# Attention loop of a macaron block on one core: the keys' correction, exponential, rounded half and remainder moved ahead of the queries' work on three engines

## The reference, cut to what matters

```python
x = x + 0.5 * ffn(layernorm(x))          # experts choose tokens: softmax over the tokens, top 8 per expert
x = x + attn(layernorm(x))
x = x + 0.5 * ffn(layernorm(x))

def attn(x):
    q, k, v = x @ Wq.T + bq, x @ Wk.T + bk, x @ Wv.T + bv      # split into 16 heads of 32
    q, k = exp(q), exp(k)
    kv = cumsum(k[:, :, :, None] * v[:, :, None, :], axis=1)
    k1 = cumsum(k, axis=1)
    num = einsum('zsD,zsDd->zsd', q, kv)
    den = sum(q * k1, axis=-1)
    return (num / den) @ Wo.T + bo
```

## Time and profile before

| | us |
|---|---|
| median of 3 runs | 2297.83 |
| lowest and highest | 2296.75, 2299.91 |
| the profiled execution, its own time | 2299.73 |
| its span | 2298.0 |
| mean granted TensorE clock over the span | 0.937 |
| busy: PE, DVE, ACT, POOL | 1981.2, 734.2, 815.3, 647.2 |

### The profile page before, as it was taken

One profiled execution on the slowest core, in us unless ns is written; L12 is line 12 of the kernel. 1 busy time (PEld: TensorE's weight loads), 2 busy tenths in 40 slices (PEclk: granted clock), 3 DMA queues, 4 the chain that ended last, 5 costly groups with the idle time before them and its releaser, 6 DMA issues.

```text
span 2298.0 us, 44195 instructions
## 1 busy us (share of the span) xinstructions
PE 1981.2 (86%) x18664; PEld 1172.0 (51%) x18664; DVE 734.2 (32%) x1248; ACT 815.3 (35%) x1525; POOL 647.2 (28%) x783
## 2 busy tenths in 40 slices
PE   5789999999999999999999999999775666656666
PEld 3546666666666666676767767766521111111111
DVE  6731111111111111467677677677410000000011
ACT  6831121111111122477777777777510000000000
POOL 7620000000000000377777777777402000000002
PEclk9899999999999999999999999999987768887788
DMA  9999999999999999366554454444699999999997
GB/s 361 346 392 401 422 428 420 422 423 419 430 418 427 420 420 397 120 221 217 158 161 149 151 161 155 151 142 157 233 412 424 427 389 428 428 427 428 428 428 335
DMA packets 113844, 762.76 MB, mean 332 GB/s; under 512 B 21736, under 2 KB 21864, under 8 KB 76016
## 3 DMA queue, kind: packets, MB, share of 16 engines
q1 hardware_dynamic: 101552, 701.35, 76.9%
q10 hardware_dynamic: 9216, 50.34, 5.3%
q0 software_dynamic: 2880, 8.25, 0.9%
HBM read 648.65 MB, written 106.43 MB: 329 GB/s over the span
## 4 chain that ended last, share of the span: by engine, by line
PE 57%; DMA 23%; POOL 8%; ACT 5%; issue 4%; SPq 1%; DVE 1%; POOLq 0%; ACTq 0%; DVEq 0%
PE ps L316 53%; DMA big<-in_L_ffn_w 22%; PE ps L320 3%; POOL big L1475 2%; POOL s L1478 2%; DMA last_scratch<-idx 1%; SPq L18 1%; POOL big L1449 1%; ACT big L600 1%; POOL s L1460 1%; ACT big L1301 1%; POOL big L1480 1%; PE ps L787 1%; ACT big L585 1%; POOL big L1472 1%
## 5 line engine op out<-in xcount | busy, mean ns | idle before, releaser
L316 PE MATMUL ps<-big 128*32 128x512 f32 (+4 forms) x13792 | 985.2, 418 | 225.7 <-DMA big<-in_L_ffn_w 183.9
L316 PEld LDWEIGHTS ps<-big 128*32 128x32 f32 (+2 forms) x13792 | 385.9, 127 | 720.3 <-issue 383.4
L324 DVE TENSOR_TENSOR big<-ps,big 128x128 f32<-128x128 f32 (+3 forms) x375 | 343.7, 931 | 676.3 <-PE ps L787 509.6
L316 PE MATMUL ps<-wth,xth 128*128 128x512 f32 x768 | 311.8, 406 | 1.5 <-DVE xtl L324 1.5
L316 PE MATMUL ps<-wtl,xth 128*128 128x512 f32 x768 | 299.6, 390 | 0.0
L316 PE MATMUL ps<-wth,xtl 128*128 128x512 f32 x768 | 299.3, 390 | 0.0
L835 ACT COPY big<-ps 128x512 f32<-128x512 f32 x64 | 37.5, 586 | 650.8 <-PE ps L316 650.8
L1467 POOL TENSOR_SCALAR big<-big 128x1 f32<-128x1 f32 x64 | 12.3, 192 | 847.3 <-ACT ps L1279 844.8
L976 ACT ACTIVATE big<-ps,big 128x512 f32<-128x512 f32 x128 | 88.2, 689 | 371.8 <-PE ps L316 359.1
L985 DVE TENSOR_SCALAR big<-ps,big 128x512 f32<-128x512 f32 x64 | 48.0, 750 | 533.7 <-PE ps L316 533.7
L316 PE MATMUL ps<-wo,s 128*128 128x512 f32 x768 | 210.1, 409 | 3.4 <-ACT big L1349 1.9
(11 more groups left out here) (128 smaller groups left out, 1753.3 us busy)
## 6 DMA issues: line engine op xcount, KB each, us to landing
big<-in_L_ffn_w SPq DMA_DIRECT2D x254, 2048.0 KB, 18.0
p_scratch<-big ACTq DMA_DIRECT2D x64, 768.0 KB, 11.0
big<-p_scratch SPq DMA_DIRECT2D x64, 768.0 KB, 5.9
big<-in_L_attn_x SPq DMA_DIRECT2D x68, 256.0 KB, 3.0
xt_scratch<-big SPq DMA_DIRECT2D x16, 1024.0 KB, 8.2
big<-xt_scratch SPq DMA_DIRECT2D x16, 1024.0 KB, 15.8
x_weight_scratch<-big SPq DMA_DIRECT2D x64, 256.0 KB, 3.3
out_x<-big SPq DMA_DIRECT2D x64, 256.0 KB, 3.6
```

What stands on the lines that cost most here:

```text
L316: return nc.tensor.matmul(o, l, r, start=start, stop=stop, skip_group_check=True)
L324: return nc.vector.tensor_tensor(o, p, q, op)
```

## The change

Three lists are reordered; no instruction is added or taken away. VectorE corrects plane 1 (k) ahead of planes 0 and 2. ScalarE takes the exponential of k first, rounds it to `KH`, and only then takes the exponential of q. GpSimd makes `KL` first, then multiplies q by `BK`. The waits go with their instructions. The lists of TensorE and SyncE stay as they are.

```diff
@@ attention_act @@
                 if nxt:
-                    act.wait_ge(s_tqv, m + 1)
+                    act.wait_ge(s_tk, m + 1)
                     act.wait_ge(s_x1rs, m + 1)
-                    nc.scalar.activation(PB[m % 4][:, 0, :], PB[m % 4][:, 0, :], ACT.Exp,
-                                         scale=RS[m % 2]).then_inc(s_qe, 1)
-                    act.wait_ge(s_tk, m + 1)
                     nc.scalar.activation(PB[m % 4][:, 1, :], PB[m % 4][:, 1, :], ACT.Exp,
                                          scale=RS[m % 2]).then_inc(s_ke, 1)
                     act.wait_ge(s_ke, m + 1)
@@
                     nc.scalar.copy(KH, PB[m % 4][:, 1, :]).then_inc(s_kh, 1)
+                    act.wait_ge(s_tqv, m + 1)
+                    nc.scalar.activation(PB[m % 4][:, 0, :], PB[m % 4][:, 0, :], ACT.Exp,
+                                         scale=RS[m % 2]).then_inc(s_qe, 1)
@@ attention_dve @@
                     dve.wait_ge(d_pb[m % 4], 16 * (m // 4 + 1))
+                    tt(PB[m % 4][:, 1, :], ps[:, 5, :], PB[m % 4][:, 1, :], ALU.add).then_inc(s_tk, 1)
                     tt(PB[m % 4][:, 0::2, :], ps[:, 4:7:2, :], PB[m % 4][:, 0::2, :], ALU.add).then_inc(s_tqv, 1)
-                    tt(PB[m % 4][:, 1, :], ps[:, 5, :], PB[m % 4][:, 1, :], ALU.add).then_inc(s_tk, 1)
@@ attention_pool @@
                     nc.gpsimd.tensor_tensor(RS[m % 2], VE[m % 2], NHALF, ALU.pow).then_inc(s_x1rs, 1)
+                    pool.wait_ge(s_kh, m + 1)
+                    pool.wait_ge(s_x1rs, m + 1)
+                    nc.gpsimd.tensor_tensor(KL, PB[j][:, 1, :], KH.bitcast(F), ALU.subtract).then_inc(s_kl, 1)
                     pool.wait_ge(s_qe, m + 1)
-                    pool.wait_ge(s_x1rs, m + 1)
+                    pool.wait_ge(s_kl, m + 1)
                     nc.gpsimd.tensor_tensor(PB[j][:, 0, :], PB[j][:, 0, :], BK, ALU.mult).then_inc(s_qb, 1)
-                    pool.wait_ge(s_kh, m + 1)
                     pool.wait_ge(s_qb, m + 1)
-                    nc.gpsimd.tensor_tensor(KL, PB[j][:, 1, :], KH.bitcast(F), ALU.subtract).then_inc(s_kl, 1)
-                    pool.wait_ge(s_kl, m + 1)
                     nc.gpsimd.tensor_tensor(X1[j], X1[j], BO, ALU.add).then_inc(s_x1b, 1)
```

## The result

The changed kernel takes **2302.94 us** (median of 20 runs, 2297.9 to 2305.1); the kernel before, run beside it, 2298.14 (20 runs, 2296.41 to 2302.09). The ratio is 1.0017 with a 95% interval of 1.0010 to 1.0023: slower by 3.9 us, 2.3 to 5.3. (The two medians alone lie 4.8 us apart; in what follows a loss or gain of the runs is worked out from the ratio, and medians are named where the two disagree.) That is inside the 0.2% and inside the range, and 1.8 us more than the forecast's +2.1. The profiled execution took 2303.43 us against 2299.73, its span 2301.7 against 2298.0.

A forecast was written before the change was run, and what follows sets the result against it. TensorE, busy 86% of the span, was taken to bound the kernel. +0.33 us per eight steps made 2.3 us over seven sequences; with -0.2 for the first, +2.1 on the median 2297.83 gave 2300.0, range 2292.0 to 2305.0.

The forecast's parts named there:

- The low keys come 0.8 us earlier: Worked in the attention's step c = 3: `KL` ready at 1427.95 instead of 1428.75, so TensorE's 0.76 us wait is gone.
- Getting `KL` 0.35 sooner lets TensorE wait later: Step c = 2: the 0.35 us gained is worth 0, since TensorE's next hard wait is for VectorE's state.
- c = 3: Attention step: L1442, now beside L405, may be held and delay L1449, which TensorE needs for q's transposes: +0.5 us.
- 0.1 us late, no more: Step c = 3: q times `BK` is ready at 1429.38, while VectorE begins to multiply by it at 1429.35.
- c = 4: Attention step: the low keys are there when TensorE comes for them, so its 0.37 us wait is gained: -0.37.
- c = 5: Attention step: GpSimd, 1.37 us late, delays ScalarE's copy L1316, which TensorE's logits need: +0.2 us.
- c = 6, 7: Long attention steps without a wait for `KL`, in which GpSimd recovers: 0.
- c = 0 and 1: Attention steps: at c = 0 the 0.35 us wait gained only lengthens TensorE's wait for L1326; at c = 1 nothing: 0.
- First sequence: No token choice beside it; GpSimd's 10.6 us turn limits after a short gain: -0.2 us, bounds -5.3 and +0.5.
- The ring that becomes the bound: Rival, chance 0.27: GpSimd's lateness is not recovered, each of seven sequences loses about 0.9 us, 6.3 in all: 2304.
- The partial gain: Rival, faster, chance 0.15: TensorE's low-key waits are partly gained, 5.3 us, 2292.5; at most 15.6 us, 2282.
- The rule of the Trainium skill: At c = 3, L1442 starting 0.02 ahead would hold L405; state and k transposes 0.6 late, some 3 us in all.

The follow-up runs named there:

- the kernels with the state first: VectorE adds the state ahead of its token choice: in the kernel before 0.9986, in the changed kernel 1.0002, in the changed kernel with GpSimd's bias moved 0.9966.
- the kernel with bias and state first: Changed kernel, GpSimd adding the output bias while waiting for ScalarE's cast and VectorE adding the state ahead of its token choice: 2290.90 us, ratio 0.9966.

## Why the prediction was right, and where not

The time (2302.94 for 2300.0, range 2292 to 2305) and the side were right. The sum had the right sign and was short by 1.8 us; several of its steps were wrong, and in the later sequences their errors cancelled, which is luck. What it was short by is the start, where TensorE's clock fell.

- **"The low keys come 0.8 us earlier", TensorE's wait vanishes:** right, 15.6 to 1.9 us. **"Getting `KL` 0.35 sooner lets TensorE wait later"** for the state: right, such waits grew from 3.3 to 11.7 us, and the kernels with the state first show it.
- **c = 3, "+0.5 us" through L1442 and L1449:** wrong. L1442 was not held (0.55 in all 64), and L1449's stay got shorter, 1.55 for 2.04. The step lost 0.22 all the same, by another path: q times `BK`.
- **"0.1 us late, no more"** for q times `BK`: this is the step that failed. I took GpSimd's start of the group as given by exponential and cast alone, and so counted the group's lateness once. But the turn is a ring: what is 0.6 late in one step is late in the next, up to the ring's 10.6 us. Where a step of before is under 10.6 (c = 0 and 7, 10.05 and 10.44), GpSimd falls back by the difference, and VectorE waited for q in 26 steps, 10.1 us, behind those two steps (at c = 1) for 0.46. I had worked out the 10.6 and used it in the first sequence only.
- **c = 4, "-0.37":** right in kind, -0.23 measured. **c = 5, "+0.2":** 0.01. **c = 6, 7:** 0 and -0.13. **c = 0 and 1, "worth 0":** +0.24 and +0.10, the same ring. The sum of a sequence, +0.33 forecast, is +0.28 in the mean of six (1.6 us in seven for 2.3): right as a sum, for partly wrong reasons.
- **First sequence, "-0.2":** wrong, +1.4, and +0.4 ahead of its first mask. Two parts of the working held. A bound ring can't go faster: the spacings of `KL` from the third on are 10.6 (10.93 once), for 10.37 to 11.03 before, and the seven steps behind the first take 0.17 less. (Some of the lateness is only handed on: the next sequence takes 0.63 more, and with the change in the first sequence alone the same seven steps take 0.28 more.) And "+0.1" for the late q at the first tile was 0.15. What the sum had at nothing is TensorE's clock at the start: it was worked out as if the full clock stayed, and the drop to 0.53 cost 1.8 us, about as much as the whole sum was short. It stands in no row of before, so it would have had to be a bound of the range.
- **The rivals.** The ring that becomes the bound came true as a mechanism, at a third of its price: 1.6 us for 6.3, because four of the eight steps are over 11 us long, and GpSimd catches up there. The partial gain needed "GpSimd's ring to have room"; the kernel with bias and state first has that room and the state out of the way, and is at 0.9966.
- **The rule of the Trainium skill** on the shared ports (page "SBUF — State Buffer", section "SBUF: two separate sides"), by which L1442, starting first, would hold L405 for its whole length: not for this small instruction, which ran beside L405 unhindered. It does hold for the 128x512 one. In the kernel with bias and state first, L1449 comes first, and VectorE is held, and then the next of GpSimd:

```profile
1425.06 1.05 POOL L1449 TENSOR_TENSOR big<-big 128x512 f32<-128x512 f32 x1 [0.22 <-DVE big L1403]
1425.21 1.97 DVE L405 SCALAR_TENSOR_TENSOR big<-big 32x1024 f32<-32x1024 f32 x1
...
1426.21 1.11 POOL L1454 TENSOR_SCALAR big<-big 128x1 f32<-128x1 f32 x1
```

L405 took 1.97 for 1.27, and L1454 1.11 for 0.27, ending at 1427.32, 0.14 behind L405. The sum of "some 3 us" that the prediction worked out by the rule is nearer to the measured 3.9 than its own 2.1, but by luck: L405 was not held by L1442 in any of the seven sequences.

Open: how often the clock drops at the attention's start in each kernel, for want of more than one profiled execution of each. No kernel tried the two tiles' order one engine at a time.

## What to carry to other kernels

Add up each engine's turn of a software pipeline as a ring: its own work, its spacings, and every wait for something that the engine itself set off in the same turn. If that sum comes near the step, a reorder that lengthens the wait inside it costs every step, however low the engine's busy share (28% here); filling the wait with work that nobody needs yet (here the bias) gives it back. A wait that goes away is worth only what lies between it and the next one, so look for the edits in twos: two worth 3.0 and 1.5 us alone gave 9.7 together. And treat the pipeline's first tiles apart, and look at TensorE's granted clock there: in the traces this order cost 2.4 us in the first two tiles and 1.0 in the other 62. Compare windows of two traces at the same place of the program, not at the same time.

## What the runs showed of the hardware

- A GpSimd instruction on 128x1 ran beside a VectorE instruction with both inputs in SBUF without either being held (0.55 and 1.27 us, seven sequences, starting 0.06 to 0.24 us ahead of it), whereas 128x512 ones held and were held: L1449 took 1.55 to 2.12 for 1.05 when L405 was first, L405 1.38 to 1.97 for 1.27 when L1449 was first. But a small one that starts while the VectorE instruction runs can be held too: L1472 1.02 for 0.55 beside L391, L1454 1.11 for 0.27.
- GpSimd's instructions, each of which here waits for the one before, start 0.07 to 0.16 us behind its end, 1.1 us in a turn of ten. One more instruction of 0.27 us, for whose result nothing waited, lengthened the turn by only 0.16 to 0.18.
- At the start of the attention TensorE's granted clock fell to 0.50 to 0.58 for 3 to 9 us in all seven traces with the new order at the first tiles, behind an idle stretch of 1.40 us; with the old order (0.79 us idle there) it fell in two of seven, some microseconds later and to 0.69 and 0.70 (windows of 3 us). In the changed kernel 64 matmuls took 2.06 us instead of 1.56 and 72 took 3.97 instead of 2.44, though TensorE had been busy for the same 3.8 of 6 us ahead of it.
